# A graph network's transfers of 125 rows cut into 112 and 13, broadcasts to 128 partitions, and two transformer layers written out

## The reference, cut to what matters

```
x = layernorm(x + gat(x))           # two graph attention layers, 8 heads, then log_softmax
x = layernorm(x + transformer(x))   # two layers as below, then a layer norm

# one graph attention layer (out_ch 128, then 64)
h = (x @ W).reshape(N, 8, out_ch)
e = leaky_relu(a_src[src] + a_dst[dst], 0.2)
alpha = segment_softmax(e, dst);  out = segment_sum(h[src] * alpha, dst) + bias

# one transformer layer (D 512, 8 heads of 64, F 256)
q, k, v = (x @ Wq.T + bq) * scale, x @ Wk.T, x @ Wv.T
w = segment_softmax((q[tgt] * k[src]).sum(-1), tgt)
x = batchnorm(x + segment_sum(w * v[src], tgt) @ Wo.T + bo)
x = batchnorm(x + relu(x @ W1.T + b1) @ W2.T + b2)
```

## Time and profile before

| | |
|---|---|
| median of three runs | 1834.06 us |
| the profiled execution's own time | 1835.38 us |
| its span, first to last instruction | 1833.6 us |
| TensorE busy | 1635.6 us (89%) |
| VectorE (DVE) busy | 1313.5 us (72%) |
| ScalarE (ACT) busy | 1171.9 us (64%) |
| GpSimd (POOL) busy | 54.0 us (3%) |
| mean granted TensorE clock | 0.941 of full speed |
| DMA | 134.06 MB, mean 73 GB/s |

### The profile page before, as it was taken

The page is one execution under the profiler, slowest core; times in us unless marked ns, Lnnn a source line. Parts: engine busy times, 40 slices in busy tenths (PEclk is TensorE's granted clock), DMA queues, the critical chain, the costliest instruction groups (busy, mean ns, idle before and its releaser), DMA issues. The chain is left out here.

```text
span 1833.6 us, 34858 instructions
## 1 busy us (share of the span) xinstructions
PE 1635.6 (89%) x14082; PEld 1511.0 (82%) x14082; DVE 1313.5 (72%) x2324; ACT 1171.9 (64%) x2108; POOL 54.0 (3%) x63
## 2 busy tenths in 40 slices
PE   6897999999979999955979999998697999999871
PEld 3786999999869999955968888888697888888870
DVE  5995999895679999953237777756632777787566
ACT  2454888897658888864337788872343778887232
POOL 0000000000000000000000000002000100000020
PEclk9999999999979999977979999998898999999985
DMA  4112122200011011004764233001266533300203
GB/s 172 54 56 92 68 83 88 80 29 1 1 64 77 29 40 45 2 21 138 210 143 116 63 96 82 13 9 50 71 158 178 133 96 84 77 29 2 57 4 115
DMA packets 71405, 134.06 MB, mean 73 GB/s; under 512 B 13829, under 2 KB 42333, under 8 KB 69956
## 3 DMA queue, kind: packets, MB, share of 16 engines
q1 hardware_dynamic: 71236, 131.73, 25.3%
HBM read 88.34 MB, written 32.01 MB: 66 GB/s over the span
## 5 line engine op out<-in xcount | busy, mean ns | idle before, releaser
L985 PE MATMUL banks<-h,probs_t_gat 125*125 125x128 f32 (+1 forms) x3200 | 373.9, 273 | 0.0
L985 PEld LDWEIGHTS banks<-h,probs_t_gat 125*125 125x125 f32 x3200 | 364.7, 190 | 0.0
L1815 DVE CUSTOM_DVE_ANT_0 probs_att<-banks,logs_or_y 125x1250 f32<-125x1250 f32 x160 | 233.6, 1460 | 147.1 <-PE banks L1719 145.5
L1775 ACT COPY probs_t_att<-banks 125x375 f32<-125x375 f32 (+1 forms) x480 | 205.7, 531 | 75.7 <-PE banks L1729 75.4
L1767 ACT ACTIVATE probs_att<-probs_att,neg_max_att 125x1250 f32<-125x1250 f32 x160 | 218.4, 1365 | 49.1 <-DVE neg_max_att L1815 49.1
L1172 DVE CUSTOM_DVE_ANT_0 probs_gat<-probs_gat,log_counts 125x1250 f32<-125x1250 f32 x160 | 232.3, 1452 | 0.1
L971 PE MATMUL banks<-ident,probs_gat 125*125 125x125 f32 x1600 | 212.4, 281 | 17.6 <-ACT probs_gat L1059 17.6
L1059 ACT ACTIVATE probs_gat<-probs_gat,neg_max_gat 125x1250 f32<-125x1250 f32 x160 | 212.6, 1329 | 15.3 <-DVE neg_max_gat L1172 14.9
L971 PEld LDWEIGHTS banks<-ident,probs_gat 125*125 125x125 f32 x1600 | 193.3, 194 | 21.0 <-ACT probs_gat L1059 21.0
L1729 PE MATMUL banks<-ident,probs_att 125*125 125x125 f32 x1600 | 191.5, 275 | 0.0
L1068 ACT COPY probs_t_gat<-banks 125x1250 f32<-125x1250 f32 x160 | 190.1, 1188 | 1.5 <-PE banks L971 1.5
(11 more groups left out here) (210 smaller groups left out, 2585.0 us busy)
## 6 DMA issues: line engine op xcount, KB each, us to landing
a_pair<-a_src_rows SPq DMA_DIRECT2D x30, 610.4 KB
logs_or_y<-log_rows SPq DMA_DIRECT2D x20, 610.4 KB
q_first<-q_rows SPq DMA_DIRECT2D x12, 1000.0 KB, 16.8
q_rows<-q_out_qkv SPq DMA_DIRECT2D x40, 250.0 KB, 4.8
q_att<-q_rows SPq DMA_DIRECT2D x8, 1000.0 KB, 17.9
log_counts<-counts_fr SPq DMA_DIRECT2D x50, 122.1 KB
k_halves<-k_low_qkv SPq DMA_DIRECT2D x20, 250.0 KB, 6.3
x_cols<-feature_cols SPq DMA_DIRECT2D x2, 2500.0 KB
```

Of the source, the lines that this page charges most:

```text
L985: total = pe.matmul(out_bank(u), probs_t[:, u % KEPT, i], rows, start=i == 0, stop=i == T - 1)
L1775: act.copy(probs_t[:, u % TURNED, lo:hi].rearrange("p c n -> p (c n)"), turned(u, j)).then_inc(piece_saved, 1)
L1815: dve.tensor_tensor_reduce(probs[:, u % SLOTS], scores, logs[:, t % KEPT], -1.0, -FLOOR, ALU.add, ALU.min, neg_max[:, column(u)]).then_inc ...
```

## The change

A new function `row_parts` cuts a number of rows at the last multiple of 16: 125 rows become rows 0 to 111 and 112 to 124. The ends of the edges (L256), the logs of the gat stage (L932), the rows of x (L957), `x_rows` (L1278), the logs' fetches (L1490, L1671), `x_pair` in and out (L1682, L1679), `x_fin` (L2110) and the output (L2119) are each moved by two DMAs instead of one, and what waits for them waits for twice the count. Broadcasts of one row, to `a_pair` (L291, L925) and to `g` (L2113), go to 128 partitions instead of 125; what reads them takes 125. The loop over layers becomes a Python loop, so that both layers stand in the code with constant addresses and names of their own. In the second layer GpSimd's bias sum and the loads and stores of `x_pair` are left out. The 125-partition broadcasts at L937, L945 and L1688, the stores of the diagonal (L276) and of the counts (L270) stay as they are.

```diff
+def row_parts(rows):
+
+    whole = rows - rows % 16
+    return ((0, whole), (whole, rows))
...
-            sp.dma_start(ends_int, ends).then_inc(ends_loaded, 16)
+            for a, b in row_parts(P):
+                sp.dma_start(ends_int[a:b], ends[a:b]).then_inc(ends_loaded, 16)
...
-                    sp.dma_start(gat.pair[:, head % 2, i], a_src_rows[i, head:head + 1, :].to_broadcast([P, N])
+                    sp.dma_start(gat.pair[:, head % 2, i], a_src_rows[i, head:head + 1, :].to_broadcast([128, N])
                                  ).then_inc(a_loaded[head % 2], 16)
...
                 for a, b in ((0, t * P), ((t + 1) * P, N)):
-                    if b > a:
-                        sp.dma_start(log_rows[own, a:b], k.log_counts[:, t, a:b]).then_inc(logs_stored, 16)
+                    for lo, hi in row_parts(P) if b > a else ():
+                        sp.dma_start(log_rows[t * P + lo:t * P + hi, a:b], k.log_counts[lo:hi, t, a:b]).then_inc(logs_stored, 16)
...
-                sp.dma_start(x_rows[t * P:(t + 1) * P, :], y[:, t, :]).then_inc(stored, 16)
-            sp.wait_ge(stored, 16 * T)
+                for a, b in row_parts(P):
+                    sp.dma_start(x_rows[t * P + a:t * P + b, :], y[a:b, t, :]).then_inc(stored, 16)
+            sp.wait_ge(stored, 32 * T)
...
             def load_logs(t):
-                sp.dma_start(logs[:, t], log_rows[t * P:(t + 1) * P, :]).then_inc(prefetched, 16)
+                for a, b in row_parts(P):
+                    sp.dma_start(logs[a:b, t], log_rows[t * P + a:t * P + b, :]).then_inc(prefetched, 16)
...
+    biased = k.layer == 0
...
             def load_x(r):
                 if r > 0:
                     sp.wait_ge(x_added, r)
-                    sp.dma_start(pair_of(x_biased, r - 1), x_pair[:]).then_inc(x_stored, 16)
-                    sp.wait_ge(x_stored, 16 * r)
+                    for a, b in row_parts(P):
+                        sp.dma_start(pair_of(x_biased, r - 1)[a:b], x_pair[a:b]).then_inc(x_stored, 16)
+                    sp.wait_ge(x_stored, 32 * r)
                 if r < T // 2:
-                    sp.dma_start(x_pair[:], pair_of(x_rows, r)).then_inc(x_loaded, 16)
+                    for a, b in row_parts(P):
+                        sp.dma_start(x_pair[a:b], pair_of(x_rows, r)[a:b]).then_inc(x_loaded, 16)
...
-                load_x(r)
+                if biased:
+                    load_x(r)
...
-                sp.dma_start(x1[:, 2 * i:2 * i + 2], x_biased.rearrange("(t p) d -> p t d", p=P)[:, 2 * i:2 * i + 2]
-                             ).then_inc(x1_loaded[i], 16)
-
-            sp.dma_start(g[:], ln_g.rearrange("(o d) -> o d", o=1).to_broadcast([P, D])).then_inc(g_loaded, 16)
+                for a, b in row_parts(P):
+                    sp.dma_start(x1[a:b, 2 * i:2 * i + 2], x_biased.rearrange("(t p) d -> p t d", p=P)[a:b, 2 * i:2 * i + 2]
+                                 ).then_inc(x1_loaded[i], 16)
+
+            sp.dma_start(g_all[:], ln_g.rearrange("(o d) -> o d", o=1).to_broadcast([128, D])).then_inc(g_loaded, 16)
...
-                sp.dma_start(out[t * P:(t + 1) * P, :], z[:, t, :]).then_inc(out_stored, 16)
-            sp.wait_ge(out_stored, 16 * T)
+                for a, b in row_parts(P):
+                    sp.dma_start(out[t * P + a:t * P + b, :], z[a:b, t, :]).then_inc(out_stored, 16)
+            sp.wait_ge(out_stored, 32 * T)
...
-        with nc.Fori(0, w["Wq"].shape[0]) as layer, ExitStack() as ctx:
+        for layer in range(w["Wq"].shape[0]):
+            k.layer = layer
+            with ExitStack() as ctx:
```

More of the change, by code:

```diff
@@ L1423, in stage_qkv @@
     SCALE = float(CH) ** -0.5
-    with k.stage("stage_qkv") as ctx:
+    with k.stage(f"stage_qkv{k.layer}") as ctx:
         def sb(what, shape, dt=F32):
-            return ctx.enter_context(nc.sbuf_tensor(f"{what}_qkv", shape, dt))
+            return ctx.enter_context(nc.sbuf_tensor(f"{what}_qkv{k.layer}", shape, dt))
         x_high, x_low = sb("x_high", [128, 2, C, W], F32R), sb("x_low", [128, 2, C, W], F32R)
@@ L1641, in stage_attend @@
         scored, masked, exp_done, sum_safe, inverted, divided, piece_turned, piece_saved, summed, att_saved = (
-            k.sem(f"{what}_att") for what in ("scored", "masked", "exp_done", "sum_safe", "inverted", "divided",
+            k.sem(f"{what}_att{k.layer}") for what in ("scored", "masked", "exp_done", "sum_safe", "inverted", "divided",
                                               "piece_turned", "piece_saved", "summed", "att_saved"))
-        block = ctx.enter_context(nc.Block("attend"))
+        block = ctx.enter_context(nc.Block(f"attend{k.layer}"))
         scores = k.psum[0:P, 0:N]
@@ L1695, in _ @@
                         load_logs(t)
-            load_x(T // 2)
-            sp.wait_ge(x_stored, 16 * (T // 2))
+            if biased:
+                load_x(T // 2)
+                sp.wait_ge(x_stored, 32 * (T // 2))
         @block.gpsimd
         def _(pool):
-            pool.wait_ge(bias_loaded, 16)
-            for r in range(T // 2):
-                pool.wait_ge(x_loaded, 16 * (r + 1))
+            if biased:
+                pool.wait_ge(bias_loaded, 16)
+            for r in range(T // 2 if biased else 0):
+                pool.wait_ge(x_loaded, 32 * (r + 1))
                 for i in range(2):
@@ L1865, in stage_tail @@
             first_normed, normed, f_summed, f_saved, f_high_done, f_low_done = (
-                k.sem(f"{what}_tl") for what in (
+                k.sem(f"{what}_tl{k.layer}") for what in (
                     "bias_loaded", "gains_loaded", "high_done",
@@ L1870, in stage_tail @@
                     "f_high_done", "f_low_done"))
-        x_loaded = [k.sem(f"x_loaded{i}_tl") for i in range(CHUNKS)]
-        block = ctx.enter_context(nc.Block("tail"))
+        x_loaded = [k.sem(f"x_loaded{i}_tl{k.layer}") for i in range(CHUNKS)]
+        block = ctx.enter_context(nc.Block(f"tail{k.layer}"))
         def nodes(s):
@@ new lines, in build @@
+        for layer in range(w["Wq"].shape[0]):
+            k.layer = layer
+            with ExitStack() as ctx:
+                Wq, Wk, Wv, Wo, W1, W2 = (w[name][layer] for name in ("Wq", "Wk", "Wv", "Wo", "W1", "W2"))
+                k_halves = ctx.enter_context(nc.sbuf_tensor(f"k_halves{layer}", [2 * CH, H, N], F32R))
+                v_rows = ctx.enter_context(nc.sbuf_tensor(f"v_rows{layer}", [P, T, D], F32))
+                y = ctx.enter_context(nc.sbuf_tensor(f"logs_or_y{layer}", [128, C, N], F32))
+                logs = y[0:P]
+                q_first = ctx.enter_context(nc.sbuf_tensor(f"q_first{layer}", [2 * CH, H, 2, 2 * P], F32R))
+                with ExitStack() as w_ctx:
+                    wq, wk, wv = (halves(nc, w_ctx, f"{name}{layer}", C, D) for name in ("wq", "wk", "wv"))
+                    stage_qkv(k, feature_cols, x_cols, (Wk, Wq, Wv), wq, wk, wv, w["bq"][layer], q_rows, q_first, k_halves, v_rows,
+                              logs, log_rows)
+                weights = weight_halves(k, ctx, f"rest{layer}_", (Wo, W1, W2))
+                stage_attend(k, q_rows, q_first, k_halves, v_rows, logs, log_rows, weights, feature_cols, x_rows,
+                             a["L1_gnn_ln_b"], x_biased)
+                stage_tail(k, feature_cols, x_cols, weights, w["bo"][layer], w["b1"][layer], w["b2"][layer],
+                           ((w["g1"][layer], w["beta1"][layer]), (w["g2"][layer], w["beta2"][layer])), y, feature_cols)
```

79 lines of the change are left out of this document (33 added, 46 removed).

## The result

| kernel | median us (lowest to highest, runs) |
|---|---|
| before | 1834.5 (1831.6 to 1837.0, 4) |
| changed | 1813.8 (1808.7 to 1817.3, 4) |

The ratio is 0.9885 [0.9854, 0.9917]: 20.7 us less. Measured a second time, the same two kernels gave 1836.5 and 1808.0, ratio 0.9841 [0.9807, 0.9875]. Forecast were 1815.0 and a range of 1808 to 1825. The profiled execution of the changed kernel took 1811.1 us, its span is 1809.3.

A forecast was written before the change was run, and what follows sets the result against it. TensorE was taken to bound the long stages, and 125-row transfers on five of sixteen DMA engines the final stage and gat_finish's end. Gains of 19.9 from 1835.4 gave 1815.5, lowered to 1815.0 us for run spread; range 1808 to 1825.

The forecast's parts named there:

- Item 1: All cut transfers: a 125-row tile of 2 KB rows falls from 2.1 us on five engines to 0.66 us.
- The term of 0.66 us a tile: Cut 125-row tiles: 8 rows, 16 KB, on an engine at 24.8 GB/s take 0.66 us.
- Item 2: End of gat_finish: stores of x_rows land earlier, so the next stage starts 8.4 us sooner; at most 10.3.
- Item 3: Final stage: no DVE wait for x_fin and no backlog of output stores; gain 7.7 us, at most 8.5.
- Item 4: Kernel start: the spread load of edge ends lets the turned weights land sooner; gain 1.3 us, between -0.4 and 2.3.
- Item 5: Turn between layers: without the loop, SP starts and issues the first weight loads sooner; gain 1.5 us, from 0 to 4.3.
- Item 6: First attend: x lands earlier, GpSimd's sum avoids DVE's division; gain 1.0 us, between -1.0 and 2.2. Second layer: 0.
- Item 7: a_pair, logs in and out, and x at L957: all hidden beside TensorE at 97%, so no gain.
- the long stages as long as before to within 1 us: Sign expected in the new profile: the long stages keep their length to within 1 us.
- Rival A: All cut transfers: 112 and 13 rows stay on few engines; 1836 us, no change; chance 0.07.
- Rival B: Second layer's three stages: written-out code stalls on instruction fetches at each start; 1829.8 us; chance 0.06.
- Rival C: gat_finish and final stage: SP's issuing becomes the bound, above 1.5 us an issue; slower, 1845 us; chance 0.04.

The follow-up runs named there:

- ends whole: The changed kernel with only the first load, of the edge ends (125 rows), made whole again; 1811.9 us, ratio 0.987.
- x and bias in both layers: The changed kernel with GpSimd's bias sum and its transfers made in both layers' attend stage, not the first alone; 1811.0 us, ratio 0.9875.
- only qkv's log loads: The kernel before with only the four log loads in each qkv stage cut into 112 and 13 rows; 1834.6 us, ratio 0.9984.

## Why the prediction was right, and where it was not

The main mechanism is shown: too few engines per transfer, with two short stages waiting for them. That 1815.0 came within 1.2 us of the first median is in part luck. The parts found one by one add up to more than the 19.9 forecast, the clock took some of it back, and the second comparison, 1808.0, stands at the lower end of the range.

- *Item 1, the price.* That 125 rows use five engines and 112 + 13 nearly all is right: shares of 0.9 and more instead of 0.3, and the 64 + 61 cut shows the single engine. The term of 0.66 us a tile was too small. In the final stage a share of 0.9 and more goes with 215 to 293 GB/s, 253 in the mean of those nine slices, about 16 GB/s for an engine, where I had taken 24.8 from 128-row loads; at 16 GB/s the 16 KB of the term take 1.0 us, not 0.66. The share times the stage's length rose from 0.30 x 47.9 = 14.4 to 0.49 x 40.3 = 19.8 us of all engines, for the same bytes. It cost nothing, for the bursts end before the next norm.
- *Item 2, `x_rows`: 8.4 forecast, 8.0 found.* Two errors nearly cancel, which is luck. The issues take 0.34 us at the median and the last ends at 828.3, no earlier than before, not at 826.9; but the last part lands 2.2 us after that, not 3.1. What is late now is the barrier behind SP, 3.4 us after ScalarE's last copy.
- *Item 3, the final stage: 7.7 forecast, 7.6 found.* The last norm ends 36.6 us after the stage's start instead of 39.3, 2.8 us earlier (3.4 forecast, since 0.9 us of the wait for the first `x_fin` stays). From there to the end of the span it takes 3.8 instead of 8.6 us, 4.8 less (4.3 forecast).
- *Item 4, the start: 1.3 forecast, 1.5 to 1.7 found* by undoing it alone, in one profile.
- *Item 5, the loop: 1.5 forecast, 2.2 to 3.2 found.* Measured from the end of ScalarE's last work in the first tail to TensorE's first matmul of the second layer, the four kernels with the loop take 10.4, 10.6, 10.2 and 10.5 us, those written out 8.0 (whole transfers) and 7.5, 7.3 and 7.6 (cut), and 7.9 and 8.1 in ends whole and in x and bias in both layers. I had put 0.6 us of SP's start and 1.0 of its four issues on the path. The issues fell to 1.77 us, below the 2.07 of the first turn that I had set as their floor, and the weights are split and used as they land. The total of the kernel with this edit alone fell by more, 3.3 to 8.3 us. Its tails, 77.5 and 77.0 us, are shorter by 3.4 and 2.2 than before. TensorE's idle time in a stage (length less busy time, both in the rows below) tells two causes apart. In the first tail it falls from 21.1 us to 17.7: that is the turn of the loop. In the second, which ends the loop, it is 17.8 and 17.6, while the granted clock is 0.87 and 0.91: that is the clock, and no gain of the edit that could be counted on. The two tails of the kernel before, then those of the one with only the layers written out:

```profile
1234.25:1315.10 80.85, 59.80 (x480) 59.26 (x480) 51.90 (x119) 21.45 (x31) 10.83 (x16) 0.90 0.14 37
1706.48:1785.67 79.19, 61.43 (x480) 60.90 (x480) 51.91 (x119) 21.45 (x30) 10.83 (x16) 0.87 0.13 33
```

```profile
1235.96:1313.43 77.47, 59.74 (x480) 59.20 (x480) 51.90 (x119) 21.45 (x30) 10.83 (x16) 0.91 0.13 34
1704.15:1781.14 76.99, 59.37 (x480) 58.83 (x480) 51.93 (x119) 21.45 (x30) 10.82 (x16) 0.91 0.13 34
```

  The kernel with a loop and a short second tail, only qkv's log loads, 77.5 us, has 0.91 there too.
- *Item 6, attend: 1.0 forecast, not resolved, and the reason doesn't hold.* In the changed kernel the meeting is gone: the first sum runs at 940.38, and no division of VectorE around it takes more than 0.87 us. But the cut did not decide that. With all transfers cut and the loop kept, the second sum meets a division of 1.99 us, and the stage takes 290.8 us, no longer than others:

```profile
955.01 1.99 DVE L1847 TENSOR_SCALAR probs_att<-probs_att,inverse_att 125x1250 f32<-125x1250 f32 x1
```

  With whole transfers, in the kernel with only the layers written out, no division beside the first sum takes more than 0.94. And the stage scatters from 290.7 to 293.4 us over kernels with the same work, more than the effect. In the second layer it is nothing, as said.
- *Item 7, "all the rest is hidden": wrong for one transfer.* This is the step that failed. I weighed the extra issues of the log loads in qkv as a possible cost, and not the loads themselves. Whole, each puts 125 KB (25 rows of 5 KB) on each of five engines, 5.0 us at 24.8 GB/s, and the stage ends with SP's wait for stores of q issued behind them. I had covered them by TensorE at 97%, which is the graph attention stage's share; here it is busy 85 of 101 us and finished before the stage's end. That the loads cost time is shown by cutting them alone, and that their bytes are still moving when the last stores of q are issued by the shares of 0.59 to 0.72 against 0.27 to 0.29. That these bytes hold up the stores on the same engines is argued from both. The cut gives 2.4 and 2.3 us when made alone, 1.8 to 2.3 a stage in the changed kernel; the extra issues cost nothing visible.

Found one by one: 8.0 + 7.6 + 1.6 + 2.8 + 4.8 = 24.8, of which item 7's 4.8 was not forecast (with the changed kernel's own qkv stages it is 3.9, and the sum 23.9). What is measured is 20.7 us the first time and about 29 the second. The two differ by as much as the largest step, and the granted clock goes with it: the changed kernel had 0.943 to 0.948 in its first four runs and 0.947 to 0.948 in the others, the kernel before 0.936 to 0.942 beside these.

**What the clock gives and takes.** Gat's instructions are the same in the kernel before and in the one with only the layers written out, and yet it takes 2.8 us longer. TensorE is mostly idle in this stage for some 10 us between 515 and 530 us, between its two halves; the granted clock falls to 0.50 (1.2 GHz) and comes back to 1.00 (2.4 GHz) at different times. The window 540 to 545 us, of the kernel before, then of the one only written out, the changed one, and the one cut 120 + 5 (the clock is the third number from the end):

```profile
540.00:545.00 5.00, 5.00 (x46) 5.00 (x45) 5.00 (x9) 3.21 (x5) 0.00 (x0) 0.95 0.33 129
```

```profile
540.00:545.00 5.00, 5.00 (x25) 5.00 (x25) 3.56 (x6) 2.54 (x4) 0.00 (x0) 0.50 0.33 128
```

```profile
540.00:545.00 5.00, 5.00 (x31) 5.00 (x30) 3.56 (x6) 2.84 (x4) 0.00 (x0) 0.62 0.01 2
```

```profile
540.00:545.00 5.00, 5.00 (x48) 5.00 (x48) 5.00 (x8) 3.89 (x7) 0.00 (x0) 1.00 0.05 8
```

PE is busy through all four, but with 25 to 48 matmuls: it does half the work at half the clock. The stages take 625.1, 627.9, 627.8 and 621.8 us, longest where the clock comes back last. Added up over windows like these from 505 to 550 us, the clock stands at 0.50 for 20.6, 27.3, 27.3 and 17.0 us. Waiting does not differ: TensorE is idle in it for 18.5 us in each of the four, as the whole stage shows, here of the kernel before and of the one cut 120 + 5 (the changed kernel's line is the first of its stages above):

```profile
174.56:799.69 625.13, 606.66 (x5136) 588.95 (x5136) 533.04 (x869) 489.92 (x776) 0.00 (x0) 0.97 0.13 46
```

```profile
173.44:795.23 621.79, 603.32 (x5136) 586.02 (x5136) 532.48 (x869) 489.48 (x776) 0.00 (x0) 0.98 0.15 46
```

So the stage's length differs by TensorE's pace alone. Two profiles of one kernel agreed to 0.01 us, and five written-out kernels with the 112-row cut or whole transfers all have 627.7 to 627.9, four with a loop 624.8 to 625.1; but the written-out one cut at 120 has 621.8. So the loop is not the cause as such; what decides the time of the clock's return stays open. It took back 2.7 us of the changed kernel's gain, and is why the prediction's line "the long stages as long as before to within 1 us" failed for gat.

Rival A (no spread) needed a flat 0.31 and 40.1 and 47.9 us in the two stages; neither is there. Rival B (stalls at stage starts) fell with ScalarE's 0.94 us at the second layer's start. Rival C (issues as the bound) needed over 1.5 us an issue; the median is 0.34 and 0.43. A slip in the chances changes nothing: 0.81 plus half of B's 0.06 is 0.84 for faster and 0.10 for the same, not 0.85 and 0.09. Of the signs named in advance two were off beside gat's: VectorE still waits 0.86 us for `x_fin`, and SP's wait for the output is 1.9 us, not about 3.

## What to carry to other kernels

Read the DMA share of a stretch in which nothing else runs, as sixteenths: a flat 5/16 said that tiles of 125 rows used five engines, and one short stage behind such a queue was worth 8 us. Cut so that both pieces divide well (112 + 13 or 120 + 5); 64 + 61 was 9% slower than that. And before calling a transfer hidden, look at what stands behind it in the same queue and who waits for that at the stage's end, rather than at how busy TensorE is in the stage.

## What the runs showed of the hardware

- A transfer of 61 rows runs at 24 to 25 GB/s, one of 125 at 121 to 128 (final stages above). At 24.8 GB/s an engine that is 1 and 5 engines. This is what the Trainium skill's page "DMA: Bandwidth & Descriptors", section "Why a DMA increments its semaphore by 16 and not by 1", gives for a prime number above 16 and for 125; the trace agrees with both. 120 + 5, by the same rule 15 and 5 engines, did as well as 112 + 13.
- Engines busy at 0.9 and more moved 215 to 293 GB/s in the final stage, with loads of 448 and 52 KB cut from `x_fin`, against 397 GB/s in a stretch of 128-row loads. Why was not tested.
- An issue on SP fell from 3.0 us at the median, with the share at a flat 3 tenths, to 0.43 with the queue drained.
- A stage of 622 to 628 us with a lull of TensorE of some 10 us in its middle moved by up to 6 us through the granted clock alone: TensorE's idle time in it was 18.5 us each time.
